# Groups of a per-element quantiser merged from the innermost outwards, over four value tiles, in a fused adapter and dense-layer kernel

## The chip, the cores and the metric

The kernel runs on one core of a Trainium2 chip. The metric is the device time of one execution in microseconds (us). TensorE is called PE (its weight loads PEld), VectorE DVE, ScalarE ACT, SyncE SP and GpSimd POOL, as in the profile.

## What is computed

The input x has 8 batches of 256 tokens with 1024 features, all in float32. Two layers follow each other:

```
# layer 0: quantise x element by element, then a mixture of 4 low-rank adapters
gi  = sum(|x| <= thresholds)             # 8 thresholds, so 0..8
idx = min(gi, 7); d = deltas[idx]; zp = zero_points[idx]
q   = (clip(round(x / d) + zp, 0, 63) - zp) * d,   but 0 where gi == 8
logits = q @ router_w.T ; gates = softmax over the best 2 of 4
x1  = x + sum over the experts of gate * (q @ A[e].T @ B[e].T) * 4
# layer 1: two dense layers, each with low-rank terms chosen per batch, one after the other
y   = x1 @ W.T + low-rank(label of the batch)
out = x1 + y @ kernel + bias + low-rank(gate of the batch) + shared low-rank
```

## The kernel before

**The products.** The two dense layers of layer 1 and the identity are multiplied with one another first: p = W.T times (kernel + shared low-rank) + identity. This takes 16 *steps* on PE (`for n in range(STEPS)`): two halves of the output columns with eight row tiles each. In the first eight steps PE has in front of the step's product a product for the per-batch low-rank part (L902, L904, the "u" product, which ACT copies out at L545). All the large products are made of three matmuls of rounded float32 parts: high by high, low by high and high by low. So every operand is split first: ACT writes the high part (for a tile of W `weight_hi`, L435), DVE subtracts to get the low part (`weight_lo`, L650, "w_lo"). Each finished step is copied from PSUM by ACT as p_hi (L533) and by DVE as p_lo (L750). Between the steps and the main part stands the product of p with the expert matrix bet (L939 to L941, 48 matmuls), which wants all p_lo parts, and bet_hi and bet_lo (L553, L763).

Then the main part: 64 more steps, numbered 16 to 79 as slots, or q = 0 to 63 in this part; eight of them for each batch b. A step of it is half of one output tile: 12 matmuls of 512 columns (L971 to L973), at its start in even steps one for the bias (L969), and in odd steps a *close* (L948, two records in the trace), in which the batch's low-rank terms (zt by tb) are added and the tile is finished. ACT then copies it out (L497) and SP stores it. In step 4 of each batch stands `z_begin` of the next one (L876, L880), and at ZEND its `z_end` (L887), whose result ACT copies to zt (L582); the close of the batch wants it.

**The quantiser.** Beside all this, ACT and DVE quantise the eight batches, one after the other, each in one piece of 128 x 2048. Per batch there are eight *groups* g, one for each threshold. ACT makes the rounded levels (`levels`, L406) and from them a clipped value (`raise_levels`, L417); DVE clips it from above and shifts it (`value`, L609), makes a mask (`mask`, L619, absx <= threshold), and merges the value into the batch's result where the mask is set (`merge`, L626). The groups go from the outermost (largest threshold) inwards, so that each overwrites the one before. At the end `finish` (L631) multiplies by absx > smallest threshold. The magnitude (L396) has one tile, absx, and waits for the `finish` of the batch before; it is made behind the raise of group 1. The tile `val` has four parts: the result of a batch is in part c % 2 (`acc`), and the values of groups 1 to 7 go round over the other two parts (`turn`). So a raise waits for the merge two groups before, and the raise of group 0 for the product of the batch two before.

PE multiplies a finished batch with the router and the adapters (`mid`, L854). DVE then ranks the logits (`order`, L691 to L700, seven small steps that each wait for the one before), ACT takes the exponential (L456), DVE makes the gates and applies them (`gate`, L707 to L713), PE turns the result round (`gated_turn`, L864), and ACT copies it to zt (`gated_out`, L462).

**The order by hand.** The engines' queues are written out in this order:

```
TAKEN = [2, 0, 2, 1, 1, 2, 1, ...]     # groups begun in each step
GROUPS[i]                              # the (batch, group) pairs of step i
DONE[c]                                # the step of batch c's last group
LAGS[c]                                # steps from DONE to mid, ranks, gate, turn, out
```

In step n DVE does first the small things (`weight_lo` for step n + 1, `p_out` of step n - 1), then GROUPS[n], then ranks and gates. In the main part ranks and gates stand ahead of the groups. ACT is one step ahead: in step n it does its small things and then levels and raises of GROUPS[n + 1].

Of the kernel before, what the change touches and what calls it, by code (L numbers as in the profile page):

```python
# [35 lines left out]
P = 128  # L36
BATCH = 8
# [26 lines left out]
def build(nc, a, out_t, itok):  # L64
# [124 lines left out]
    abs_made, levels_made, raised = sem("abs_made"), sem("levels_made"), sem("raised")  # L189
    valued, masked, merged, q_made = sem("valued"), sem("masked"), sem("merged"), sem("q_made")  # L190
    mid_made, gate_step, gap_made, exp_made = sem("mid_made"), sem("gate_step"), sem("gap_made"), sem("exp_made")
# [17 lines left out]
    AHEAD = 2  # L209
    LAGS = [(2, 3, 4, 5, 6)] * 2 + [(2, 4, 5, 6, 7)] * (BATCH - 4) + [(1, 2, 3, 4, 5)] * 2  # L210
    TAKEN = [2, 0, 2, 1, 1, 2, 1, 1, 1, 1, 1, 1, 1, 1, 1, 2, 1, 1]
    ORDER = [(c, g) for c in range(BATCH) for g in range(G)]
    SLOTS = STEPS + BATCH * KT
    LAST = STEPS + BATCH * KT - 8
    rest, room = len(ORDER) - AHEAD - sum(TAKEN), LAST + 1 - len(TAKEN)
# [5 lines left out]
    DONE = [max([-1] + [i for i in range(SLOTS) if (c, G - 1) in GROUPS[i]]) for c in range(BATCH)]  # L221
    MID, RANK, GATE, TURN, OUT = {}, {}, {}, {}, {}
    for c, d in enumerate(DONE):
        mid_at, rank_at, gate_at, turn_at, out_at = LAGS[c]
        MID[d + mid_at], RANK[d + rank_at], GATE[d + gate_at], TURN[d + turn_at] = c, c, c, c

        OUT[d + out_at if c < ZSLOTS else max(d + out_at, STEPS + (c - ZSLOTS + 1) * KT)] = c
# [32 lines left out]
    def slot(b, j):  # L260
        return STEPS + b * KT + j

    def acc(c):

        return c % 2

    def turn(c, g):

        return acc(c) if g == 0 else 2 + g % 2

# [3 lines left out]
    with nc.allow_non_contiguous_dma(reason="rows of 1 KB and small constants"), nc.Block() as block:  # L274
# [117 lines left out]
        def _(act):  # L392
            def magnitude(c):
                if c:
                    act.wait_ge(q_made, c)
                nc.scalar.activation(absx, xq[:, c % 2], ACT.Abs).then_inc(abs_made, 1)  # L396

            def levels(c, g):

                if g == 0 and c == 0:  # L400
                    act.wait_ge(x_first_in, 16)
                elif g == 0:
                    act.wait_ge(xq_in[c % 2], 16 * ((c + 1) // 2))
                if c * G + g >= 2:
                    act.wait_ge(raised, c * G + g - 1)
                nc.scalar.activation(level[:, g % 2], xq[:, c % 2], ACT.Copy, scale=inv[:, g:g + 1]).then_inc(levels_made, 1)  # L406

            def raise_levels(c, g):

                act.wait_ge(levels_made, c * G + g + 1)  # L410
                if g == 0 and c >= 2:
                    act.wait_ge(mid_made, c - 1)
                elif g >= 3:
                    act.wait_ge(merged, c * (G - 1) + g - 2)
                elif c and g:
                    act.wait_ge(merged, c * (G - 1) + 1 - g)
                nc.scalar.activation(val[:, turn(c, g)], level[:, g % 2], ACT.Relu, bias=shift[:, g:g + 1],  # L417
                                     scale=par[:, 1, g:g + 1]).then_inc(raised, 1)
# [116 lines left out]
            for n in range(STEPS):  # L535
# [39 lines left out]
            for q in range(BATCH * KT + LAG + 1):  # L575
# [17 lines left out]
                if slot(b, j) in RANK:  # L593
                    gate_exp(RANK[slot(b, j)])
                if b + 1 < BATCH and j in XAT:
# [8 lines left out]
        def _(dve):  # L604
            def value(c, g):

                dve.wait_ge(raised, c * G + g + 1)
                v = val[:, turn(c, g)]
                nc.vector.tensor_scalar(v, v, width[:, g:g + 1], unshift[:, g:g + 1], ALU.min, ALU.add).then_inc(valued, 1)  # L609

            def mask(c, g):

                if g == 1:
                    dve.wait_ge(abs_made, c + 1)
                    if c:
                        dve.wait_ge(merged, c * (G - 1))
                elif g >= 3:
                    dve.wait_ge(merged, c * (G - 1) + g - 2)
                nc.vector.tensor_scalar(inside[:, g % 2], absx, thr[:, g - 1:g], None, ALU.is_le).then_inc(masked, 1)  # L619

            def merge(c, g):
                dve.wait_ge(valued, c * G + g + 1)
                dve.wait_ge(masked, c * (G - 1) + g)
                if g >= 2:
# [60 lines left out]
            def order(c):  # L685
# [16 lines left out]
            def gate(c):  # L702

                n = c * GATE_STEPS
                mid = midbank[:, 0:TT * RT].rearrange("p (t m) -> p t m", t=TT)
                dve.wait_ge(exp_made, c + 1)
                then(nc.vector.scalar_tensor_tensor(gates, rank, TOP_K, expo, ALU.is_lt, ALU.mult), n + 8)  # L707
                then(nc.vector.reduce_sum(total, gates, AX), n + 9)
# [75 lines left out]
        def _(pe):  # L784
# [61 lines left out]
            def mid(c):  # L846

                pe.wait_ge(q_made, c + 1)
                pe.wait_ge(ra_in, 16)
# [182 lines left out]
```

## Time and profile before

| what | us |
|---|---|
| median of 3 runs | 481.31 (480.68 to 481.42) |
| the profiled execution | 477.87 |
| its span | 476.1 |
| PE busy | 461.1 |
| DVE busy | 392.2 |
| ACT busy | 358.1 |

The granted clock of PE was 1.00 of full speed throughout, so 2.4 GHz. A bracket at the end of a timeline row gives the idle time of that engine just before the instruction, and what ended it.

### The profile page before, as it was taken

Reading aid. Unit: us, or ns where it says so; the run is one execution under the profiler, and the core shown is the slowest. Engines: PE = TensorE matmul, PEld = TensorE weight load, DVE = VectorE, ACT = ScalarE, POOL = GpSimd, SP = SyncE. Lnnn points to the kernel's source line nnn. Section 1 sums busy time; section 2 is a strip of 40 time slices with the busy share of each in tenths; the row PEclk is TensorE's granted clock in tenths of the full one; section 3 lists DMA queues with packets and bytes.
Section 4 is the critical chain, followed back from the end, with each engine's and each line's share of the span. In section 5 each row is a group of like instructions: output and inputs, shape, how many; then the busy total and the mean of one; then the engine's idle time right before and its main releaser. Section 6 shows DMA issues by size and latency. Waiting matters only on the chain.

```text
span 476.1 us, 5627 instructions
## 1 busy us (share of the span) xinstructions
PE 461.1 (97%) x2182; PEld 352.9 (74%) x2182; DVE 392.2 (82%) x381; ACT 358.1 (75%) x299; POOL 5.6 (1%) x11
## 2 busy tenths in 40 slices
PE   8899989999999899999999999999999999989896
PEld 8537878888688777777777777787778768857774
DVE  1376889897999989996999799999989995999600
ACT  1499977893799986579789959968989778968002
POOL 0000010000000000000000000000000000000000
PEclk9999999999999999999999999999999999999999
DMA  8998323302143222605035106304304104101102
GB/s 270 362 361 339 75 64 136 99 12 67 43 164 124 89 45 88 200 0 156 11 134 154 56 1 187 112 1 155 144 8 149 55 1 132 56 1 44 45 0 89
DMA packets 35836, 50.35 MB, mean 106 GB/s; under 512 B 26626, under 2 KB 26882, under 8 KB 33538
## 3 DMA queue, kind: packets, MB, share of 16 engines
q1 hardware_dynamic: 34802, 42.66, 27.9%
q0 software_dynamic: 1008, 7.34, 4.1%
q8 instruction: 17, 0.28, 0.2%
q14 instruction: 9, 0.07, 0.0%
HBM read 39.51 MB, written 10.49 MB: 105 GB/s over the span
## 4 chain that ended last, share of the span: by engine, by line
PE 73%; DVE 14%; issue 4%; ACT 4%; DMA 3%; SPq 1%; DVEq 0%; ACTq 0%
PE bank L971 11%; PE bank L973 10%; PE bank L972 10%; DVE val L626 7%; PE bank L854 5%; PE bank L948 5%; PE bank L880 5%; PE bank L919 4%; PE bank L923 4%; PE bank L920 4%; PE bank L902 4%; DMA kst<-k_in 3%; PE bank L811 3%; DVE inside L619 3%; DVE val L609 2%
## 5 line engine op out<-in xcount | busy, mean ns | idle before, releaser
L417 ACT ACTIVATE val<-level,shift,small 128x2048 f32<-128x2048 int16 x64 | 133.9, 2093 | 16.2 <-DVE val L626 16.1
L626 DVE COPY_PREDICATED val<-inside,val 128x2048 f32<-128x2048 uint8 x56 | 142.8, 2550 | 0.3
L406 ACT ACTIVATE level<-xq,inv 128x2048 int16<-128x2048 f32 x64 | 127.9, 1999 | 0.8
L971 PE MATMUL bank<-p_hi,x_hi 128*128 128x512 f32 x256 | 101.8, 398 | 0.0
L973 PE MATMUL bank<-p_hi,x_lo 128*128 128x512 f32 x256 | 100.0, 391 | 0.0
L972 PE MATMUL bank<-p_lo,x_hi 128*128 128x512 f32 x256 | 99.9, 390 | 0.0
L609 DVE TENSOR_SCALAR val<-val,width,unshift 128x2048 f32<-128x2048 f32 x64 | 87.3, 1366 | 13.9 <-ACT val L417 13.5
L619 DVE TENSOR_SCALAR inside<-absx,thr 128x2048 uint8<-128x2048 f32 x56 | 72.1, 1300 | 3.9 <-ACT absx L396 3.9
L971 PEld LDWEIGHTS bank<-p_hi,x_hi 128*128 128x128 f32 x256 | 48.1, 188 | 17.0 <-issue 8.4
L973 PEld LDWEIGHTS bank<-p_hi,x_lo 128*128 128x128 f32 x256 | 48.1, 188 | 10.4
L972 PEld LDWEIGHTS bank<-p_lo,x_hi 128*128 128x128 f32 x256 | 48.1, 188 | 10.1 <-issue 0.2
L919 PE MATMUL bank<-kp_hi,w_hi 128*128 128x512 f32 x128 | 51.3, 401 | 3.1 <-DVE w_lo L650 3.1
L923 PE MATMUL bank<-kp_hi,w_lo 128*128 128x512 f32 x128 | 50.3, 393 | 0.0
L920 PE MATMUL bank<-kp_lo,w_hi 128*128 128x512 f32 x128 | 49.9, 390 | 0.0
L948 PE MATMUL bank<-tb,zt 128*128 128x512 f32 x64 | 32.6, 600 | 1.3 <-ACT zt L582 1.3
L854 PEld LDWEIGHTS bank<-ra,val 128*128 128x128 f32 x256 | 29.7, 192 | 3.9 <-DVE val L631 2.3
L854 PE MATMUL bank<-ra,val 128*128 128x68 f32 x256 | 29.6, 274 | 1.8 <-DVE val L631 1.8
L919 PEld LDWEIGHTS bank<-kp_hi,w_hi 128*128 128x128 f32 x128 | 24.1, 188 | 8.3 <-DVE w_lo L650 3.8
L902 PE MATMUL bank<-aefft,wst 128*128 128x256 f32 x128 | 29.1, 380 | 0.6 <-ACT ust L545 0.6
L880 PE MATMUL bank<-xs,ub 128*64 128x256 f32 x128 | 29.3, 382 | 0.0
L902 PEld LDWEIGHTS bank<-aefft,wst 128*128 128x128 f32 x128 | 24.1, 190 | 5.1 <-issue 1.7
L923 PEld LDWEIGHTS bank<-kp_hi,w_lo 128*128 128x128 f32 x128 | 24.0, 188 | 5.2
(91 smaller groups left out, 459.8 us busy)
## 6 DMA issues: line engine op xcount, KB each, us to landing
xs<-xt_in SPq DMA_DIRECT2D x8, 1024.0 KB, 4.9
out_t<-ost SPq DMA_DIRECT2D x16, 512.0 KB, 3.0
wst<-w_in SPq DMA_DIRECT2D x14, 512.0 KB, 3.5
xq<-xt_in POOLq DMA_DIRECT2D x7, 1024.0 KB, 6.1
la<-la_in SPq DMA_DIRECT2D x4, 512.0 KB, 5.3
lb<-lb_in SPq DMA_DIRECT2D x4, 512.0 KB, 12.7
kst<-k_in SPq DMA_DIRECT2D x4, 512.0 KB, 16.1
kst<-k_in SPq DMA_DIRECT2D x1, 2048.0 KB, 9.0
```

Source lines behind the costliest of these rows:

```text
L406: nc.scalar.activation(level[:, g % 2], xq[:, c % 2], ACT.Copy, scale=inv[:, g:g + 1]).then_inc(levels_made, 1)
L417: nc.scalar.activation(val[:, turn(c, g)], level[:, g % 2], ACT.Relu, bias=shift[:, g:g + 1], scale=par[:, 1, g:g + 1]).then_inc(raised, 1)
L609: nc.vector.tensor_scalar(v, v, width[:, g:g + 1], unshift[:, g:g + 1], ALU.min, ALU.add).then_inc(valued, 1)
L619: nc.vector.tensor_scalar(inside[:, g % 2], absx, thr[:, g - 1:g], None, ALU.is_le).then_inc(masked, 1)
L626: nc.vector.copy_predicated(val[:, acc(c)], inside[:, g % 2], val[:, turn(c, g)]).then_inc(merged, 1)
L854: last = mm(midbank[:, t * RT:(t + 1) * RT], val[:, acc(c), k, t * P:(t + 1) * P], ra[:, k], start=k == 0, stop=k == KT - 1)
L902: mm(ubank, wst[n % 2][:, o], aefft[:, o], start=o == 0, stop=False)
L919: mm(obank[n % RING], w_hi[side(n)][:, o], kp_hi[:, o], start=o == 0, stop=False)
L923: last = mm(obank[n % RING], w_lo[side(n)][:, o], kp_hi[:, o], start=False, stop=o == KT - 1)
L971: mm(o, x_hi[:, s, k, at], p_hi[:, h, k], start=False, stop=False)
L972: mm(o, x_hi[:, s, k, at], p_lo[:, h, k], start=False, stop=False)
L973: last = mm(o, x_lo[:, s, k, at], p_hi[:, h, k], start=False, stop=False)
```

## The change

**Merging.** Group g now works with threshold, delta and zero point 7 - g (`group`), so the innermost comes first. Masks are absx > threshold: each group overwrites what lies outside its own inner bound. The multiplication by absx > smallest threshold is done at once to the value of group 0 (`begin`, the same operation as `finish` was). The mask for group g + 1 is made in group g. The magnitude of batch c is made behind the raise of its group 0 and waits for the last mask of the batch before.

**Tiles.** All four parts of `val` go round. `HOMES[c]` names the part of batch c's result, and three for the other groups: three of the four, since the batch before is kept until its product. Its part is taken by group 3, whose raise waits for that product (mid_made >= c). From group 4 on a raise waits for the merge three before.

**Ranks.** The seven small steps of `order` are written so that two that don't depend on each other follow without a wait; best is taken from PSUM instead of from lg.

**Order.** TAKEN and LAST are changed; the lags stay (the exponential has one of its own, equal to that of the ranks). The groups of the steps, where they differ:

```
step          0        1    3    4        5        6
before   0.2 0.3       -   0.6  0.7      1.0 1.1  1.2
after    0.2          0.3   -   0.6 0.7  1.0      1.1 1.2
step         14       15       16
before      2.2    2.3 2.4    2.5
after        -     2.2 2.3    2.4 2.5
last group of batches 0 to 7, before: 4 11 19 30 40 51 62 72
                              after:  4 11 19 29 40 50 61 71
```

So the products of batches 3, 5, 6 and 7 come one step sooner. Batch 7's groups 1 to 7 are in steps 64, 66, 67, 68, 70, 71, 72 before, and in 64, 65, 66, 68, 69, 70, 71 after.

```diff
-    LAGS = [(2, 3, 4, 5, 6)] * 2 + [(2, 4, 5, 6, 7)] * (BATCH - 4) + [(1, 2, 3, 4, 5)] * 2
-    TAKEN = [2, 0, 2, 1, 1, 2, 1, 1, 1, 1, 1, 1, 1, 1, 1, 2, 1, 1]
+    LAGS = [(2, 3, 3, 4, 5, 6)] * 2 + [(2, 4, 4, 5, 6, 7)] * (BATCH - 4) + [(1, 2, 2, 3, 4, 5)] * 2
+    TAKEN = [1, 1, 2, 0, 2, 1, 2, 1, 1, 1, 1, 1, 1, 1, 0, 2, 2, 1]
-    LAST = STEPS + BATCH * KT - 8
+    LAST = STEPS + BATCH * KT - 9
...
+    HOMES = [[0, 1, 2, 3]]
+    for c in range(1, BATCH):
+        first, second, third, fourth = HOMES[-1]
+        HOMES.append([third, fourth, second, first])
+
     def acc(c):
-        return c % 2
+        return HOMES[c][0]
     def turn(c, g):
-        return acc(c) if g == 0 else 2 + g % 2
+        return HOMES[c][0 if g == 0 else 1 + (g - 1) % 3]
+    def group(g):
+        return slice(G - 1 - g, G - g)
...
             def magnitude(c):
                 if c:
-                    act.wait_ge(q_made, c)
+                    act.wait_ge(masked, c * (G - 1))
...
             def raise_levels(c, g):
-                if g == 0 and c >= 2:
-                    act.wait_ge(mid_made, c - 1)
-                elif g >= 3:
-                    act.wait_ge(merged, c * (G - 1) + g - 2)
-                elif c and g:
-                    act.wait_ge(merged, c * (G - 1) + 1 - g)
+                if g == 3 and c:
+                    act.wait_ge(mid_made, c)
+                elif g >= 4:
+                    act.wait_ge(merged, c * (G - 1) + g - 3)
+                elif c and g < 3:
+                    act.wait_ge(merged, c * (G - 1) + g - 2)
...
-                if c and g == 1:
+                if c and g == 0:
                     magnitude(c)
...
-                if n in RANK:
-                    gate_exp(RANK[n])
+                if n in EXP:
+                    gate_exp(EXP[n])
...
-                nc.vector.tensor_scalar(inside[:, g % 2], absx, thr[:, g - 1:g], None, ALU.is_le).then_inc(masked, 1)
+                nc.vector.tensor_scalar(inside[:, g % 2], absx, thr[:, group(g)], None, ALU.is_gt).then_inc(masked, 1)
...
-            def finish(c):
-
-                dve.wait_ge(merged, (c + 1) * (G - 1))
-                nc.vector.scalar_tensor_tensor(val[:, acc(c)], absx, thr[:, G - 1:G], val[:, acc(c)],
-                                               ALU.is_gt, ALU.mult).then_inc(q_made, 1)
+            def begin(c):
+
+                dve.wait_ge(valued, c * G + 1)
+                dve.wait_ge(abs_made, c + 1)
+                nc.vector.scalar_tensor_tensor(val[:, acc(c)], absx, thr[:, group(0)], val[:, acc(c)],
+                                               ALU.is_gt, ALU.mult).then_inc(begun, 1)
 
             def quant(c, g):
                 value(c, g)
-                if g == 1:
-                    mask(c, 1)
-                if g and g + 1 < G:
+                if g == 0:
+                    begin(c)
+                if g + 1 < G:
                     mask(c, g + 1)
                 if g:
                     merge(c, g)
-                if g + 1 == G:
-                    finish(c)
...
-                then(nc.vector.tensor_copy(lg, mid[:, :, ER:RT]), n + 1)
-                then(nc.vector.reduce_max(best, lg, AX), n + 2)
-                nc.vector.tensor_tensor(gap, lg, best.unsqueeze(2).to_broadcast([P, TT, E]), ALU.subtract).then_inc(gap_made, 1)
-                then(nc.vector.tensor_tensor(ties, other, mine, ALU.is_equal), n + 3)
-                then(nc.vector.tensor_tensor(ties, ties, before, ALU.mult), n + 4)
-                then(nc.vector.tensor_tensor(beats, other, mine, ALU.is_gt), n + 5)
-                then(nc.vector.tensor_tensor(beats, beats, ties, ALU.add), n + 6)
-                then(nc.vector.reduce_sum(rank, beats, AX), n + 7)
+                nc.vector.tensor_copy(lg, logits).then_inc(gate_step, 1)
+                nc.vector.reduce_max(best, logits, AX).then_inc(gate_step, 1)
+                dve.wait_ge(gate_step, n + 1)
+                nc.vector.tensor_tensor(ties, other, mine, ALU.is_equal).then_inc(gate_step, 1)
+                nc.vector.tensor_tensor(beats, other, mine, ALU.is_gt).then_inc(gate_step, 1)
+                dve.wait_ge(gate_step, n + 2)
+                nc.vector.tensor_tensor(gap, lg, best.unsqueeze(2).to_broadcast([P, TT, E]), ALU.subtract).then_inc(gap_made, 1)
+                dve.wait_ge(gate_step, n + 3)
+                nc.vector.tensor_tensor(ties, ties, before, ALU.mult).then_inc(gate_step, 1)
+                dve.wait_ge(gate_step, n + 5)
+                nc.vector.tensor_tensor(beats, beats, ties, ALU.add).then_inc(gate_step, 1)
+                dve.wait_ge(gate_step, n + 6)
+                nc.vector.reduce_sum(rank, beats, AX).then_inc(gate_step, 1)
...
-            value(0, 0)
-            mask(0, 1)
-            mask(0, 2)
-            value(0, 1)
-            merge(0, 1)
+            quant(0, 0)
+            quant(0, 1)
             weight_lo(1)
...
-                pe.wait_ge(q_made, c + 1)
+                pe.wait_ge(merged, (c + 1) * (G - 1))
```

## Rows read from the trace of the kernel before

**Rows 1.** The page's first part: busy time, share of the span, instructions.
```profile
PE 461.1 (97%) x2182; PEld 352.9 (74%) x2182; DVE 392.2 (82%) x381; ACT 358.1 (75%) x299; POOL 5.6 (1%) x11
```

**Rows 2.** Busy time by stretch: length, PE, PEld, DVE, ACT, POOL, clock, DMA.
```profile
232.00:268.00 36.00, 36.00 (x172) 27.21 (x171) 34.88 (x23) 33.36 (x24) 0.53 (x1) 1.00 0.30 99
```

**Rows 3.** Timeline of PE: start, length, line, operation; in brackets the idle time before.
```profile
47.48 2.83 PE L902 MATMUL bank<-aefft,wst 128*128 128x256 f32 x12 [0.57 <-ACT ust L545]
...
62.88 0.50 PE L919 MATMUL bank<-kp_hi,w_hi 128*128 128x512 f32 x1 [1.56 <-DVE w_lo L650]
...
157.37 0.50 PE L919 MATMUL bank<-kp_hi,w_hi 128*128 128x512 f32 x1 [1.58 <-DVE w_lo L650]
...
162.99 3.68 PE L854 MATMUL bank<-ra,val 128*128 128x68 f32 x32
...
178.64 0.50 PE L939 MATMUL bank<-p_hi,bet_hi 128*128 128x512 f32 x1 [0.99 <-DVE bet_lo L763]
...
189.96 0.50 PE L939 MATMUL bank<-p_hi,bet_hi 128*128 128x512 f32 x1 [0.83 <-DVE p_lo L750]
...
413.98 0.71 PE L864 MATMUL bank<-ident,mg 128*128 128x128 f32 x4 [0.19 <-DVE mg L713]
...
422.45 1.98 PE L948 MATMUL bank<-tb,zt 128*128 128x512 f32 x4 [1.26 <-ACT zt L582]
...
446.71 3.45 PE L854 MATMUL bank<-ra,val 128*128 128x68 f32 x29 [1.83 <-DVE val L631]
```

**Rows 4.** Groups of instructions: busy us, mean ns | idle before, releasers.
```profile
L626 DVE COPY_PREDICATED val<-inside,val 128x2048 f32<-128x2048 uint8 x56 | 142.8, 2550 | 0.3
L417 ACT ACTIVATE val<-level,shift,small 128x2048 f32<-128x2048 int16 x64 | 133.9, 2093 | 16.2 <-DVE val L626 16.1
...
L609 DVE TENSOR_SCALAR val<-val,width,unshift 128x2048 f32<-128x2048 f32 x64 | 87.3, 1366 | 13.9 <-ACT val L417 13.5
L619 DVE TENSOR_SCALAR inside<-absx,thr 128x2048 uint8<-128x2048 f32 x56 | 72.1, 1300 | 3.9 <-ACT absx L396 3.9
...
L631 DVE SCALAR_TENSOR_TENSOR val<-absx,thr,val 128x2048 f32<-128x2048 f32 x8 | 18.8, 2352 | 0.3
```

**Rows 5.** Timeline of DVE in the 16 steps.
```profile
47.89 1.25 DVE L650 TENSOR_TENSOR w_lo<-wst,w_hi 128x1024 fp32r<-128x1024 f32 x1
...
56.17 1.36 DVE L609 TENSOR_SCALAR val<-val,width,unshift 128x2048 f32<-128x2048 f32 x1
...
61.57 1.26 DVE L650 TENSOR_TENSOR w_lo<-wst,w_hi 128x1024 fp32r<-128x1024 f32 x1
...
156.10 1.22 DVE L650 TENSOR_TENSOR w_lo<-wst,w_hi 128x1024 fp32r<-128x1024 f32 x1
...
177.36 1.23 DVE L763 TENSOR_TENSOR bet_lo<-bet,bet_hi 128x1024 fp32r<-128x1024 f32 x1 [0.19 <-ACT bet_hi L553]
...
189.23 0.68 DVE L750 TENSOR_TENSOR p_lo<-bank,p_hi 128x512 fp32r<-128x512 f32 x1
```

**Rows 6.** Timeline of ACT in the 16 steps.
```profile
55.15 1.05 ACT L435 ACTIVATE w_hi<-wst 128x1024 fp32r<-128x1024 f32 x1
...
175.80 0.58 ACT L533 ACTIVATE p_hi<-bank 128x512 fp32r<-128x512 f32 x1
```

**Rows 7.** The chain of waits around batch 6's product: start, length, what.
```profile
394.16 0.86 PE bank L948 x2
...
401.58 3.54 PE bank L854 x32
```

**Rows 8.** Timeline of DVE in the ranks of batch 6.
```profile
405.14 0.17 DVE L691 COPY lg<-bank 128x8 f32<-128x8 f32 x1 [5.22 <-PE bank L854]
...
405.54 0.17 DVE L693 TENSOR_TENSOR gap<-lg,best 128x8 f32<-128x8 f32 x1
405.62 0.18 DVE L696 TENSOR_TENSOR ties<-lg 128x32 f32<-128x32 f32 x1
405.84 0.19 DVE L697 TENSOR_TENSOR ties<-ties,before 128x32 f32<-128x32 f32 x1
```

More of the change, by code:

```diff
@@ L189, in build @@
     abs_made, levels_made, raised = sem("abs_made"), sem("levels_made"), sem("raised")
-    valued, masked, merged, q_made = sem("valued"), sem("masked"), sem("merged"), sem("q_made")
+    valued, begun, masked, merged = sem("valued"), sem("begun"), sem("masked"), sem("merged")
     mid_made, gate_step, gap_made, exp_made = sem("mid_made"), sem("gate_step"), sem("gap_made"), sem("exp_made")
@@ L221, in build @@
     DONE = [max([-1] + [i for i in range(SLOTS) if (c, G - 1) in GROUPS[i]]) for c in range(BATCH)]
-    MID, RANK, GATE, TURN, OUT = {}, {}, {}, {}, {}
+    MID, RANK, EXP, GATE, TURN, OUT = {}, {}, {}, {}, {}, {}
     for c, d in enumerate(DONE):
-        mid_at, rank_at, gate_at, turn_at, out_at = LAGS[c]
-        MID[d + mid_at], RANK[d + rank_at], GATE[d + gate_at], TURN[d + turn_at] = c, c, c, c
+        mid_at, rank_at, exp_at, gate_at, turn_at, out_at = LAGS[c]
+        MID[d + mid_at], RANK[d + rank_at], EXP[d + exp_at], GATE[d + gate_at], TURN[d + turn_at] = c, c, c, c, c
         OUT[d + out_at if c < ZSLOTS else max(d + out_at, STEPS + (c - ZSLOTS + 1) * KT)] = c
@@ L405, in levels @@
                     act.wait_ge(raised, c * G + g - 1)
-                nc.scalar.activation(level[:, g % 2], xq[:, c % 2], ACT.Copy, scale=inv[:, g:g + 1]).then_inc(levels_made, 1)
+                nc.scalar.activation(level[:, g % 2], xq[:, c % 2], ACT.Copy, scale=inv[:, group(g)]).then_inc(levels_made, 1)
             def raise_levels(c, g):
                 act.wait_ge(levels_made, c * G + g + 1)
-                if g == 0 and c >= 2:
-                    act.wait_ge(mid_made, c - 1)
-                elif g >= 3:
+                if g == 3 and c:
[3 more added lines that the diff above has]
+                elif c and g < 3:
                     act.wait_ge(merged, c * (G - 1) + g - 2)
-                elif c and g:
-                    act.wait_ge(merged, c * (G - 1) + 1 - g)
-                nc.scalar.activation(val[:, turn(c, g)], level[:, g % 2], ACT.Relu, bias=shift[:, g:g + 1],
-                                     scale=par[:, 1, g:g + 1]).then_inc(raised, 1)
+                nc.scalar.activation(val[:, turn(c, g)], level[:, g % 2], ACT.Relu, bias=shift[:, group(g)],
+                                     scale=par[:, 1, group(g)]).then_inc(raised, 1)
             def quant(c, g):
@@ L592, in _ @@
                         quant(c, g)
-                if slot(b, j) in RANK:
-                    gate_exp(RANK[slot(b, j)])
+                if slot(b, j) in EXP:
+                    gate_exp(EXP[slot(b, j)])
                 if b + 1 < BATCH and j in XAT:
@@ L608, in value @@
                 v = val[:, turn(c, g)]
-                nc.vector.tensor_scalar(v, v, width[:, g:g + 1], unshift[:, g:g + 1], ALU.min, ALU.add).then_inc(valued, 1)
+                nc.vector.tensor_scalar(v, v, width[:, group(g)], unshift[:, group(g)], ALU.min, ALU.add).then_inc(valued, 1)
             def mask(c, g):
                 if g == 1:
-                    dve.wait_ge(abs_made, c + 1)
                     if c:
@@ L623, in merge @@
                 dve.wait_ge(masked, c * (G - 1) + g)
-                if g >= 2:
+                if g == 1:
+                    dve.wait_ge(begun, c + 1)
+                else:
                     dve.wait_ge(merged, c * (G - 1) + g - 1)
                 nc.vector.copy_predicated(val[:, acc(c)], inside[:, g % 2], val[:, turn(c, g)]).then_inc(merged, 1)
-            def finish(c):
-                dve.wait_ge(merged, (c + 1) * (G - 1))
-                nc.vector.scalar_tensor_tensor(val[:, acc(c)], absx, thr[:, G - 1:G], val[:, acc(c)],
-                                               ALU.is_gt, ALU.mult).then_inc(q_made, 1)
+            def begin(c):
[3 more added lines that the diff above has]
+                                               ALU.is_gt, ALU.mult).then_inc(begun, 1)
             def quant(c, g):
                 value(c, g)
-                if g == 1:
-                    mask(c, 1)
-                if g and g + 1 < G:
+                if g == 0:
+                    begin(c)
+                if g + 1 < G:
                     mask(c, g + 1)
@@ L690, in order @@
                 dve.wait_ge(before_in, 16)
-                then(nc.vector.tensor_copy(lg, mid[:, :, ER:RT]), n + 1)
-                then(nc.vector.reduce_max(best, lg, AX), n + 2)
-                nc.vector.tensor_tensor(gap, lg, best.unsqueeze(2).to_broadcast([P, TT, E]), ALU.subtract).then_inc(gap_made, 1)
+                logits = mid[:, :, ER:RT]
                 mine = lg.unsqueeze(3).to_broadcast([P, TT, E, E])
                 other = lg.unsqueeze(2).to_broadcast([P, TT, E, E])
-                then(nc.vector.tensor_tensor(ties, other, mine, ALU.is_equal), n + 3)
-                then(nc.vector.tensor_tensor(ties, ties, before, ALU.mult), n + 4)
-                then(nc.vector.tensor_tensor(beats, other, mine, ALU.is_gt), n + 5)
-                then(nc.vector.tensor_tensor(beats, beats, ties, ALU.add), n + 6)
-                then(nc.vector.reduce_sum(rank, beats, AX), n + 7)
+                nc.vector.tensor_copy(lg, logits).then_inc(gate_step, 1)
[11 more added lines that the diff above has]
+                nc.vector.reduce_sum(rank, beats, AX).then_inc(gate_step, 1)
             def gate(c):
@@ L706, in gate @@
                 dve.wait_ge(exp_made, c + 1)
+                dve.wait_ge(gate_step, n + 7)
                 then(nc.vector.scalar_tensor_tensor(gates, rank, TOP_K, expo, ALU.is_lt, ALU.mult), n + 8)
```

## The prediction

> **What bounds the kernel now.** I read the page's first part, then the waits of PE alone, then the timelines of PE, DVE and ACT around each of them, and last the chain of waits near the end.
>
> PE is busy for 461.1 of 476.1 us [rows 1]. In the middle it never rests: 36.00 of 36.00 us in the stretch shown [rows 2], and its clock is full. So the time is PE's own work plus the few places where it stands. The change leaves PE's work as it is; all that it can win is in those places. There are eight after the first 25 us [rows 3], and the reader should see their releasers: 0.57 for a copy of ACT, 1.56 and 1.58 for a low part of the weights (w_lo), 0.99 for bet_lo, 0.83 for p_lo, 0.19 for mg, 1.26 for zt, 1.83 for the finished batch 7 (val L631). Together 8.81. The rest of the 15.0 us without PE work lies in the first 23 us and in the last store, which the change doesn't touch.
>
> They have one cause: DVE or ACT has the quantiser's work in front of a small step that PE wants.
>
> **The change, part by part.**
>
> (1) *The work of the quantiser stays.* Per batch there are still 8 levels, 8 raises and one magnitude on ACT, and 8 values, 7 masks, 7 merges and one multiply by absx > thr on DVE. Means are in [rows 4]; the multiply (2.35 us) goes from the end of a batch (finish) to its start (begin). is_gt for is_le costs nothing: same form and tiles. Merges with dense and with sparse masks are all among the 56 of one group with mean 2550 ns, so turning the masks around costs nothing either; I bound it by the 0.15 us by which single merges differ, times the 7 of the last batch, 1 us to either side.
>
> (2) *The first wait for w_lo, 1.56.* Now step 0 has groups 0.2 and 0.3, and only then comes step 1's w_lo at 61.57 [rows 5]. PE wanted it at 62.88 less 1.56, at 61.3. After the change step 0 has 0.2 alone. DVE is free at 56.17, adds the k part (0.6), and the high part is there from 55.15 + 1.05 = 56.2 [rows 6]: w_lo is made by 58.0. Gain 1.56, with 3 us to spare. In the prelude DVE has the multiply more and one mask is moved, so w_lo of tile 1, now at 47.89 [rows 5], is begun about 1.1 later and made at 50.2 (after raise(0,1), at 44.1, come a value, a mask and a merge, 4.85, and w_lo itself, 1.25); PE wants it 3.9 after 47.48, at 51.4: 1.2 us to spare. The 0.57 stays: ACT's order there is the same.
>
> (3) *The second, 1.58.* DVE makes w_lo at 156.10, right after finish(1) [rows 5]. Finish is gone from there: 2.3 us (2.35 long, [rows 4]). All of DVE's steps before it hang on PE's and come 1.56 sooner with it, and the ranks of batch 0 save 0.4 (below). So it is made at 157.3 - 2.3 - 1.6 - 0.4 = 153.0; PE, itself 1.56 sooner, wants it at 155.8 - 1.56 = 154.2. Gain 1.58, with 1.2 to spare. What is behind: group 2.0 now has multiply and mask too, 3.5 us more ahead of the w_lo of step 14, which is made by 159.3; PE wants it only after its step 13, 5.6 (157.37 to 162.99, [rows 3]), and the product of batch 1, 3.5, so at 163.4.
>
> (4) *bet_lo, 0.99, and p_lo, 0.83.* Step 14 loses its group, so DVE has ranks, p_lo(14) and bet_lo as soon as PE's step 14 is over (163.4 + 5.6 = 169.0). bet_lo then takes 0.3 until ACT copies, 1.56 from ACT's copy at 175.80 to bet_lo at 177.36 and its own 1.23 [rows 5, 6]: 172.1, wanted at 174.6. Then two groups (4.85 each: 56.17 to 61.57 less the 0.6 of the k part) and the gate (1.0), and p_lo(15) is made at 183.4, where it now is made at 189.9 [rows 5]. PE wants it for its last three of 48 products of 0.23 us each (5.6 over the 24 of a step), so 10.2 after 174.6, at 184.8. Gain 1.82, with 1.4 to spare. ACT has to give raise(2,3) for that, which now also waits for batch 1's product (163.4): it is reached at about 166, so no wait. Up to here 4.96 us.
>
> (5) *Middle.* The products of batches 3, 5, 6 and 7 are asked one step sooner. Between the ranks of one batch and the product of the next DVE has six groups: at most 6/8 of a batch's (142.8+87.3+72.1+18.8)/8 = 40.1 [rows 4], 30.1, plus ranks and gate 2.6 and two x_lo 2.5: 35.2. PE needs 39.2 for ten steps (next point). So 4 us to spare, and no new wait; ACT's waits for merges (16.1 us, [rows 4]) get shorter with the third turning tile, but these lie beside PE's work and are worth nothing there.
>
> (6) *The end.* From the end of batch 6's product, 401.58 + 3.54 = 405.12 [rows 7], to batch 7's at 446.71 [rows 3] are 41.6 us: ten steps of PE, 38.3, and waits of 0.19, 1.26 and 1.83. DVE was ready early (5.22 idle before 405.14, [rows 8]) and then worked without a break to 446.66. After the change the stretch begins one step sooner. PE has one close more in it, 0.86 [rows 7]: 39.2. DVE has 41.5 less 2.35 (finish) less 1.20 (first mask, now in group 7.0, which fills the 5.22): 38.0. The ranks save 0.4, but with no group between them the gate waits about 0.4 for ACT's exp. So DVE is done 1.2 us before PE asks: 1.83 goes. The gate follows the ranks at once and has three steps until its turn: 0.19 goes. zt is copied in a step of ACT that now has no group ahead of it: 1.26 goes. ACT's raise(7,4) now comes after that copy, and this is the tightest point: PE's four steps with turn and z_end take 13.3, zt 0.4, a level and a raise 4.0, so 17.7 from the start of the stretch; DVE wants it after ranks and gate (2.6), three groups (14.6) and an x_lo (1.1), at 18.3. Gain 3.28.
>
> (7) *Ranks.* Two operations with a wait between start 0.22 apart (405.62 to 405.84), two without 0.08 (405.54 to 405.62) [rows 8]. Three of the seven waits lose their effect, so 0.4 us per batch.
> The Trainium skill (VectorE: DVE Perf Modes, The DRAIN you can't avoid) says that leaving semaphores out between chained VectorE operations gains nothing, and that the semaphore itself is free. By it the ranks would stay at 1.6 us and the two margins of 1.2 us would be 0.8; the sum is the same by either. The rows just named disagree with it for such small tiles.
>
> **Sum:** 1.56 + 1.58 + 0.99 + 0.83 + 0.19 + 1.26 + 1.83 = 8.24. The profiled execution took 477.87 (span 476.1); it would take 469.6. The median of the runs, 481.31, is 3.4 above it, and I take the same difference off it: 473.1.
>
> **Rivals.**
>
> *A, one of the tight places holds:* margins are 1.2 (tile 1), 1.2 (step 13), 1.4 (p_lo), 0.6 (raise(7,4)) and 1.2 (batch 7). Hand sums like these err by a microsecond or two. DVE late by 2 to 4 us in the last stretch would give back 1 to 3 us of the 8.24, w_lo late by as much again up to 1.6: 474.3 to 477.5, say 475.5. For it: five places with little room. Against: each alone would have to lose its margin first, and what it gives back is only what goes beyond it. Chance 0.27.
>
> *B, slower: the products asked too early.* Place: batches 3, 5, 6 and 7 on PE. If ACT, held at raise(c,3), which now waits for the product of the batch before, starves DVE, then this product is late, and the next raise with it. Price: a step is 3.3 us on average (two from 394.16 + 0.86 = 395.02 to 401.58, [rows 7]); four times this is 13.1, less the 8.24: 486.2. It decides from where DVE is more than 4 us later than PE's step (point 5). Against: ACT comes to raise(c,3) one to three steps after the product except in step 6, where it may wait 1 us with nothing of PE's behind. Chance 0.05.
>
> *C, nothing changes: DVE is the bound.* DVE's and ACT's busy shares are 82% and 75% [rows 1]; weight loads fill only 74% of PE's time. If PE had slack within its busy time, the fixed sum of DVE's work would set the time and reordering would bring nothing: 481.3. Against: the middle stretch, where PE takes 36.00 of 36.00 and DVE idles.
> The Trainium skill (Perfetto Trace Analysis, Identifying the Most-Contended Engine) reads PE by its weight loads, not by its matmuls' busy share. By that rule this case comes true; the trace doesn't bear it out, as PE restarts at once on each release. Chance 0.06.
>
> *D, more than the sum:* restarts after a wait cost PE some 0.1 to 0.2 us each beyond the idle time (first matmuls of 0.50 where others take 0.40), and DVE's early lead might take the 0.57 too: up to 1.5 more, 471.6. Chance 0.10.
>
> The forecast itself has 0.52.
>
> **How the numbers follow.** 473.1 is the likeliest. The range from 471.7 to 477.0 holds the forecast, D and most of A, and leaves out B, C and the end of A. About 0.2% (1 us) is what a measurement of this kernel can tell from no change. Faster by more: forecast, A, D and a little less, 0.88; within it: C, 0.06; slower: B, 0.06.
>
> **What would show it right or wrong.** PE's waits should be four: three in the first 23 us and the 0.57 at 47. No wait for w_lo at 61 and 154, none before bet_hi's products, none for zt; the product of batch 7 starts at about 435 without a wait; DVE idles less than 2 us between batch 6's product and it. PE's busy time stays within 1 us of 461. Wrong would be: a wait of PE for val L626 (A or B), for w_lo whose releaser is ACT's w_hi (A), waits of ACT for PE's product L854 ahead of L417 (B), or PE's busy time growing by what its waits lose (C).

## The result, and the profile after

The kernel after takes 468.28 us (467.90 to 468.35, 4 runs), the kernel before 481.37 in the same comparison: ratio 0.9725, interval 0.969 to 0.976, so 13.1 us less. Forecast were 473.1 and 8.2 less, with a range down to 471.7. The direction was right, the size was not, and the time lies below the range.

Page of after, parts 1 and 2 (busy time, share of the span, instructions; below, tenths of full clock in 40 slices):

```profile
span 466.1 us, 5628 instructions
...
PE 459.5 (99%) x2182; PEld 353.3 (76%) x2182; DVE 389.0 (83%) x381; ACT 356.8 (77%) x299; POOL 5.4 (1%) x11
...
PEclk9999999999999999999999999999999999999999
```

Beside [rows 1] the span is 10.0 us shorter, DVE and ACT do what they did (DVE 3 us less, most of it the ranks: with the old ones it is 391.6), and PE's busy time is 1.6 less, beyond the 1 us that the prediction allowed. These are all of PE's waits in after (engine, line, waited for: us in total, times, longest):

```profile
PE bank L802 <- DVE warm L675: 1.2, 1, 1.2
PE bank L814 <- DVE kst L667: 1.0, 1, 1.0
PE bank L915 <- ACT ust L554: 0.7, 1, 0.7
```

Of the eight waits in [rows 3] only the first is left, the 0.57, now 0.68; the prediction had a third wait in the first 23 us, of which two are left. The groups of [rows 4] in after:

```profile
L636 DVE COPY_PREDICATED val<-inside,val 128x2048 f32<-128x2048 uint8 x56 | 142.3, 2542 | 0.3
L426 ACT ACTIVATE val<-level,shift,small 128x2048 f32<-128x2048 int16 x64 | 133.9, 2091 | 2.3 <-PE bank L867 1.9
...
L618 DVE TENSOR_SCALAR val<-val,width,unshift 128x2048 f32<-128x2048 f32 x64 | 86.0, 1344 | 9.5 <-ACT val L426 9.5
```

The merge costs what it cost (2542 ns for 2550), with the masks turned round. ACT's raise waited 16.1 us for merges and now waits for one merge, 0.4; the other 1.9 is for PE's product L867 of the batch before. The last stretch, timeline of DVE and of PE in after, answers to [rows 8] and the last of [rows 3]:

```profile
395.56 0.17 DVE L703 COPY lg<-bank 128x8 f32<-128x8 f32 x1 [2.70 <-PE bank L867]
395.64 0.15 DVE L704 TENSOR_REDUCE best<-bank 128x2 f32<-128x8 f32 x1
395.76 0.19 DVE L706 TENSOR_TENSOR ties<-lg 128x32 f32<-128x32 f32 x1
...
396.50 0.18 DVE L715 TENSOR_REDUCE rank<-beats 128x8 f32<-128x32 f32 x1
...
430.59 2.48 DVE L636 COPY_PREDICATED val<-inside,val 128x2048 f32<-128x2048 uint8 x1
```
```profile
434.10 3.68 PE L867 MATMUL bank<-ra,val 128*128 128x68 f32 x32
```

DVE is done at 433.07, 37.5 after the stretch begins, and PE asks at 434.10, 38.5 after: 1.0 to spare.

The span lost 10.0 us, the waits only 8.24. Where the rest lies can be read from the starts of the same matmuls before and after. The first matmuls of steps 1 and 2, before and then after:

```profile
51.37 0.47 PE L919 MATMUL bank<-kp_hi,w_hi 128*128 128x512 f32 x1
62.88 0.50 PE L919 MATMUL bank<-kp_hi,w_hi 128*128 128x512 f32 x1 [1.56 <-DVE w_lo L650]
```
```profile
51.17 0.48 PE L932 MATMUL bank<-kp_hi,w_hi 128*128 128x512 f32 x1
60.90 0.48 PE L932 MATMUL bank<-kp_hi,w_hi 128*128 128x512 f32 x1
```

The same work takes 11.51 us before and 9.73 after, so the wait shown as 1.56 was worth 1.78. The whole span, cut at such starts:

| stretch | before, us | after, us | less by | waits in it before |
|---|---|---|---|---|
| up to step 1 | 51.37 | 51.17 | 0.20 | (0.57, stays) |
| step 1 to step 2 | 11.51 | 9.73 | 1.78 | 1.56 |
| to step 13 | 94.49 | 92.74 | 1.75 | 1.58 |
| to the product with bet | 21.27 | 19.94 | 1.33 | 0.99 |
| to the main part | 17.48 | 16.58 | 0.90 | 0.83 |
| to the end | 279.97 | 275.96 | 4.01 | 0.19, 1.26, 1.83 |

From step 1 on that is 9.8 us for waits of 8.24: 1.5 more over seven places, some 0.2 for each stop. Stretches without a wait are as long as before (steps 2 to 8: 64.16 and 64.15). PE's ends are modelled, so how much of it counts as busy is open; the starts aren't.

### The profile page after: what moved, and what is told of

The parts are those of the page before. It is cut to its first block, busy times and chain, and to the rows that moved or that the text cites. A ratio compares the mean times of both kernels' runs of the same rounds, so it can differ in the third digit from the quotient of the medians.

```text
span 466.1 us, 5628 instructions
## 1 busy us (share of the span) xinstructions
PE 459.5 (99%) x2182; PEld 353.3 (76%) x2182; DVE 389.0 (83%) x381; ACT 356.8 (77%) x299; POOL 5.4 (1%) x11
## 4 chain that ended last, share of the span: by engine, by line
PE 87%; ACT 4%; DMA 3%; DVE 2%; issue 2%; SPq 1%; ACTq 0%
PE bank L984 13%; PE bank L986 13%; PE bank L985 13%; PE bank L961 6%; PE bank L893 6%; PE bank L867 5%; PE bank L915 5%; PE bank L936 5%; PE bank L932 5%; PE bank L933 5%; DMA kst<-k_in 3%; PE bank L824 3%; PE bank L889 2%; PE bank L982 2%; ACT level L415 1%
## 5 line engine op out<-in xcount | busy, mean ns | idle before, releaser
L636 DVE COPY_PREDICATED val<-inside,val 128x2048 f32<-128x2048 uint8 x56 | 142.3, 2542 | 0.3
L618 DVE TENSOR_SCALAR val<-val,width,unshift 128x2048 f32<-128x2048 f32 x64 | 86.0, 1344 | 9.5 <-ACT val L426 9.5
L867 PEld LDWEIGHTS bank<-ra,val 128*128 128x128 f32 x256 | 29.7, 192 | 1.4 <-issue 1.0
L867 PE MATMUL bank<-ra,val 128*128 128x68 f32 x256 | 29.5, 273 | 0.0
L933 PEld LDWEIGHTS bank<-kp_lo,w_hi 128*128 128x128 f32 x128 | 24.1, 188 | 5.0 <-issue 0.2
```

The source lines that it names most:

```text
L618: nc.vector.tensor_scalar(v, v, width[:, group(g)], unshift[:, group(g)], ALU.min, ALU.add).then_inc(valued, 1)
L867: last = mm(midbank[:, t * RT:(t + 1) * RT], val[:, acc(c), k, t * P:(t + 1) * P], ra[:, k], start=k == 0, stop=k == KT - 1)
L933: mm(obank[n % RING], w_hi[side(n)][:, o], kp_lo[:, o], start=False, stop=False)
```

## Where the other 5 us came from: the kernel before, profiled again

The sum of the prediction was made against one profiled execution of 477.87 us. The first question was what its distance to the median is.

> The kernel before, unchanged, profiled again. Its profiled execution on record took 477.9 us, its other executions 480.7 to 482.9. Theory 1 (the ordinary execution of before has more or longer waits of PE than the one profiled): a second profile has a span of about 479.5 and PE waits for DVE and ACT that add up to some 3 us more than the 8.8 after the first 25 us, PE busy still 461. Theory 2 (the difference is PE's own pace, the transfers or the chip): the same eight waits with the same lengths, and the time lies in PE's busy time, in the first 25 us or in the clock. Theory 3: the span is 476 again and the difference lies outside the span.

Measured: span 480.7, mean clock 0.989. PE's waits are the same eight, with the same lengths within 0.12 us. PE's busy time is 466.1 instead of 461.1, and the place is one. Timeline of PE, then busy time by stretch (length, PE, PEld, DVE, ACT, POOL, granted clock, DMA):

```profile
446.47 6.35 PE L854 MATMUL bank<-ra,val 128*128 128x68 f32 x32 [1.76 <-DVE val L631]
```
```profile
440.00:446.40 6.40, 4.72 (x21) 3.57 (x19) 6.33 (x4) 0.00 (x0) 0.00 (x0) 1.00 0.20 82
446.40:457.00 10.60, 10.53 (x43) 9.56 (x44) 2.33 (x14) 0.21 (x1) 0.00 (x0) 0.54 0.01 2
457.00:470.00 13.00, 13.00 (x58) 10.20 (x57) 0.00 (x0) 0.76 (x2) 0.00 (x0) 0.98 0.00 1
```

After PE has waited for the finished batch 7, the clock falls from 2.4 to 1.2 GHz. The product of 32 short matmuls takes 6.35 us. The clock is back after 10.2 us; half of these are lost. In the execution on record the same wait of 1.83 was followed by full clock, and the product took 3.79 (the row in [rows 3] shows only 29 of its 32 matmuls).

Each execution's record has its mean clock, and the comparisons of this and the later runs have 51 executions of the kernel before. One, at 0.982 and 486.25 us, stands apart from the other 50. By clock: 8 at 1.00, median 478.1 us; 3 at 0.996, 479.9; 26 at 0.992 or 0.993, median about 481.3; 13 at 0.989, median 482.9. The 0.989 is the case profiled here, 10.2 us at half clock; a mean of 0.993 over 480 us is worth 0.007 x 480 / 0.5 = 6.7 us of it, and 0.996 half as much. The profile on record was of the rare kind, at full clock. Theory 2 holds: not more waits, but the clock. Between executions at full clock, 478.1 and 468.3, the change is worth 9.8 us; the other 3.3 are what the median of before has on top. Where the clock fell in the executions at 0.992 and 0.993 no profile shows; that it is the same place follows only from the next two runs.

The Trainium skill (TensorE: Matmul & The Clock Gate, Part 1) describes these two levels and a monitor of activity that sets them. The levels agree with the profile: 0.50 and 1.00 of full speed.

## Is it that one wait? Taken away from before, put into after

```diff
-    LAGS = [(2, 3, 4, 5, 6)] * 2 + [(2, 4, 5, 6, 7)] * (BATCH - 4) + [(1, 2, 3, 4, 5)] * 2
+    LAGS = [(2, 3, 4, 5, 6)] * 2 + [(2, 4, 5, 6, 7)] * (BATCH - 4) + [(1, 2, 3, 4, 5), (2, 3, 4, 5, 6)]
```

> The kernel before with batch 7's product and all that hangs on it one step later, nothing else. Theory (the clock): PE's wait of 1.8 us ahead of that product is what lets the granted clock fall to half for 6.8 or 10.2 us in 19 of 23 executions so far, at a cost of 3.4 or 5.1 us on top. Without the wait the clock stays at 1.00 in every execution and the median falls from 481 to 474.5 to 475, 6 us for a wait of 1.8. Rival: the clock falls for the sum of PE's pauses, or whatever it does there: it still falls in most executions, and the median is 1.8 less, about 479.

Measured: 475.72 us (475.23 to 477.56, 6 runs), ratio 0.989 (0.985 to 0.993), clock 1.00 in five and 0.996 in one. In that one, which was profiled, the 3.4 us at half clock lie between 25 and 30 us of the span, among the start's products, not at the end. The wait before batch 7's product is gone and the other seven stand. A wait of 1.8 us was worth 5.7 in the median: 2.4 between executions at full clock (478.1 and 475.7), the rest lost clock. The theory holds. (The expectation counts 19 of 23 executions with a fall; the record has 18.)

The reverse: after, with DVE work ahead of batch 7's last merge (masks that nobody reads).

```diff
             def quant(c, g):
...
+                if (c, g) == (7, G - 1):
+                    dve.wait_ge(merged, c * (G - 1) + g - 1)
+                    dve.wait_ge(valued, c * G + g + 1)
+                    for i, n in enumerate([KT] * 2 + [2]):
+                        nc.vector.tensor_scalar(inside[:, 0, 0:n], val[:, turn(c, g), 0:n], 0.0, None, ALU.is_gt).then_inc(spent, 1)
+                        dve.wait_ge(spent, i + 1)
                 if g:
                     merge(c, g)
```

> The kernel after with 2.8 us of DVE work added ahead of the last merge of batch 7 (masks of a value that nobody reads). DVE had 1.0 us to spare there, so PE waits about 1.8 us for the product. Theory (the clock): it falls to half there in most executions, median 468.3 + 1.8 + 3.4 = 473.5 or more, single ones at 470.1 with clock 1.00. Rival (the fall needs the other waits of before too): all executions at 470.1.

Measured: 474.52 us (473.52 to 475.37, 6 runs), clock 0.989 or 0.993 in all six. PE's timeline, and the stretch behind the wait:

```profile
436.32 6.66 PE L874 MATMUL bank<-ra,val 128*128 128x68 f32 x32 [1.85 <-DVE val L637]
```
```profile
436.80:447.10 10.30, 10.30 (x40) 9.38 (x40) 2.00 (x13) 0.69 (x2) 0.00 (x0) 0.50 0.13 52
```

So the added DVE work (2.95 us in the trace) cost 6.2, of which 1.85 is the wait. With less work (`[KT] + [2]`):

> As the kernel with a wait of 1.85 us ahead of batch 7's product, but with 1.6 us of added DVE work instead of 2.8: a wait of about 0.6 us. Theory (length of the pause matters): the clock stays at 1.00 in most executions, median 468.9. Rival (any pause just ahead of the short matmuls does it): clock 0.989 to 0.993, median 472 or more.

Measured: 469.61 us (468.63 to 472.22, 6 runs), wait 0.61, clock 0.998 or more in four, 0.996 and 0.993 in the others. The profiled one is that at 0.996, and its fall lies before 30 us again (23.3 to 26.7). So the pause's length matters at this place: a third of it mostly kept the clock. The same work ahead of the last merge of batch 1 (`[KT] * 2 + [6]`) makes PE wait at a place where full matmuls follow:

> The kernel after with 3.4 us of the same DVE work ahead of the last merge of batch 1, so that w_lo of step 13 comes late: PE waits about 2 us ahead of a step of full matmuls. In before no execution seen lost its clock after such a wait (1.56 and 1.58). Theory (it matters what follows: after the wait for batch 7 come 32 short matmuls of 68 columns, here 24 of 512): clock 1.00, median 468.3 + 2.0 = 470.3. Rival (any pause of 1.8 us or more does it): clock below 1, median 473.5. If the p_lo or bet_lo waits come back by less than 1 us, that is the margin of the prediction's point 4 used up.

Measured: 472.99 us (470.70 to 474.02, 6 runs). The wait is 2.49, longer than meant (w_lo comes 3.5 us later, and in after it had only 0.8 to spare), and the clock was 1.00 in two executions, 0.996 in three, 0.993 in one. The profiled one is at 1.00 and has full clock right behind the wait:

```profile
156.38 0.50 PE L939 MATMUL bank<-kp_hi,w_hi 128*128 128x512 f32 x1 [2.49 <-DVE w_lo L666]
```

Neither theory holds as stated. A longer pause than batch 7's cost less clock here. Where the clock fell in the other four executions isn't shown, as only one is profiled. It need not be behind this wait: kernels without any such wait also have executions at 0.996 or 0.993 (two of four with the old ranks, below).

All the profiles together say more than this run alone. Eleven pauses of 1.5 to 2.7 us stand ahead of products of 512 columns (w_lo and bet_lo, in seven profiles), and no fall of the clock begins behind any of them. Of the four pauses of 1.76 to 2.41 ahead of batch 7's product three were followed by one. So was each of two pauses for p_lo, of 1.85 and 1.79 in two kernels of the next section; behind these stand three matmuls of 512 columns and then 32 of 64 and 256. The place matters, then, and it isn't what PE did just before: ahead of step 13 and ahead of batch 7's product alike it had been at 512 columns. What it is in the short matmuls (their columns, or their weight loads) was not separated. It isn't the pauses of before at 414 and 422 [rows 3] either: the kernel with the 1.85 has none of them.

## The parts of the change by themselves

**The order alone** (TAKEN and LAST of after; merging, tiles and ranks of before):

```diff
-    TAKEN = [2, 0, 2, 1, 1, 2, 1, 1, 1, 1, 1, 1, 1, 1, 1, 2, 1, 1]
+    TAKEN = [1, 1, 2, 0, 2, 1, 2, 1, 1, 1, 1, 1, 1, 1, 0, 2, 2, 1]
-    LAST = STEPS + BATCH * KT - 8
+    LAST = STEPS + BATCH * KT - 9
```

> The kernel before with TAKEN and LAST of after, merging, tiles and ranks as before. If the parts add up as in the prediction's steps: the first w_lo wait (1.56), bet_lo and p_lo (1.82) and zt and mg (1.45) go; the second w_lo wait stays at about 1.5, since finish(1) is still ahead of it; the wait for batch 7's product stays and is 2 to 2.5 us, since DVE has 41.5 us of work there against 39.2 of PE. Profiled span about 471 to 472, ratio to before about 0.990. Rival (handing out the groups does all of it): as after, ratio 0.973. Rival (order is worth nothing without the new merging): 1.00.

Measured: 490.36 us (488.80 to 490.90, 4 runs), ratio 1.020 (1.013 to 1.026): slower than before by 9. Two waits came where they were expected, 2.27 for w_lo of step 13 (about 1.5 expected) and 2.41 for batch 7. The 1.85 for p_lo was expected to be gone. A fourth was in no sum. Timelines of ACT and PE:

```profile
190.60 1.99 ACT L406 ACTIVATE level<-xq,inv 128x2048 int16<-128x2048 f32 x1
198.40 2.09 ACT L417 ACTIVATE val<-level,shift,small 128x2048 f32<-128x2048 int16 x1 [5.81 <-DVE val L626]
200.52 1.08 ACT L486 ACTIVATE tb<-bank 64x512 f32<-64x512 f32 x2
201.50 0.21 ACT L478 ACTIVATE bu<-bank 64x64 f32<-64x64 f32 x1
```
```profile
201.76 1.11 PE L887 MATMUL bank<-zt,bu 64*64 64x256 f32 x2 [5.21 <-ACT bu L478]
```

ACT is at raise(2,6), the raise of batch 2's group 6, which wants the merge two groups before, and DVE, with groups 2.2 and 2.3 later than before, hasn't come to it. Behind the raise stands the copy of bu, which z_end multiplies, and PE waits 5.21 for it. The p_lo is late in the same way: ACT's p_hi of step 15 stands behind raise(2,5), at 186.23 to 188.33. Around the wait for bu the clock falls too:

```profile
196.00:202.00 6.00, 0.79 (x4) 0.34 (x3) 6.00 (x4) 3.29 (x4) 0.00 (x0) 0.94 0.90 298
202.00:210.00 8.00, 8.00 (x25) 5.83 (x25) 5.86 (x4) 2.46 (x5) 0.00 (x0) 0.62 0.04 7
```

It is at half for 6.8 us there, from 201.3, just before PE starts again; for 3.4 us from 191.0, behind the wait for p_lo; and for 6.8 us from 453.9, behind that for batch 7. Half of that, some 8 us, is lost. Against before's profiled execution at full clock the span is 12.0 longer, so most of it is clock.

**The new order without the third turning tile** (the tile stays, the raises wait as if there were two):

```diff
                 elif g >= 4:
-                    act.wait_ge(merged, c * (G - 1) + g - 3)
+                    act.wait_ge(merged, c * (G - 1) + g - 2)
```

> The kernel after with the raises of groups 4 to 7 waiting for the merge two before, as with two turning tiles, all else as after. The prediction said that the third turning tile is worth nothing on PE. But the new order with the old tiles had ACT stand 5.8 us at raise(2,6) for merge(2,4), behind it bu, and PE waited 5.2 for bu. Theory (the tile carries the new order): this wait comes back here, PE waits some 3 to 5 us ahead of z_end(0), and the clock may fall after it; ratio 0.985 to 1.00. Rival (the tile is worth nothing, what hurt there was finish): as after, ratio 0.973.

Measured: 479.90 us (478.34 to 481.93, 10 runs), ratio 0.997 (0.994 to 1.000); waits of 5.24 for bu and 1.79 for p_lo, no other after 50 us, clock 0.985 to 0.993. In the profiled one it is at half for 3.4 us behind the wait for p_lo and for 6.8 us around that for bu. So one part of `val` carries 11.6 us of after's time, 7 of them waits and most of the rest clock. Under the old order of groups it is another matter. First the new merging and all tiles with the old order:

> The kernel after with TAKEN and LAST of before: new merging, four tiles and new ranks alone. By the prediction's steps: the first w_lo wait (1.56) and most of bet_lo and p_lo (1.8) stay, the second w_lo wait, zt and the wait for batch 7's product go (1.58, 1.26, 1.83). Profiled span about 471, ratio about 0.990. If instead the product of batch 7 is still waited for, the DVE sum of the last stretch (38 us) is wrong. Rival (merging alone does all): ratio 0.973.

Measured: 473.16 us (472.62 to 473.68, 4 runs), ratio 0.985 (0.978 to 0.991), clock 0.999 or more in all. Span 470.8 as expected; these waits are left after 50 us and the ones for the second w_lo and for batch 7 are gone:

```profile
PE bank L932 <- DVE w_lo L659: 1.5, 1, 1.5
...
PE bank L952 <- DVE bet_lo L776: 1.2, 1, 1.2
PE bank L952 <- DVE p_lo L763: 0.9, 1, 0.9
...
PE bank L961 <- ACT zt L591: 0.2, 1, 0.2
```

And the same with the line above at g - 2:

> New merging with the old order of groups, raises of groups 4 to 7 waiting for the merge two before. With the third turning tile this order had a span of 470.8. Theory (the tile carries the new order only; under the old one it saves ACT waits that PE never sees): span within 0.5 of 470.8, no wait for bu, ratio 0.984. Rival (the tile is worth as much here as under the new order): PE waits for bu, ratio near 1.00.

Measured: 474.38 us (473.91 to 475.16, 4 runs), span 472.8. No wait for bu. But 2.0 in the span where I expected under 0.5: the wait for bet_lo is 2.73 instead of 1.18, as ACT's bet_hi stands behind such a raise as well (it waits 2.36 at 174 us), and 0.5 more lies in the first 37 us, which the tile doesn't touch. So the tile is worth 1.2 (medians) to 1.4 us under the old order and 11.6 under the new.

**The small parts.** After with LAST of before:

> The kernel after with LAST of before (groups of batch 7 over one step more, its product a step later). By the prediction's sums DVE and PE are level in the last stretch either way. The old-order run had only a wait of 0.2 for zt there, so: span 466.3, median as after within 0.3. Rival: the earlier product is what keeps the clock up or hides zt, and this is 1 us or more slower.

Measured: 468.63 us (468.29 to 470.68, 4 runs), span 466.5, a wait of 0.24 for zt: level with after. After with the old ranks:

> The kernel after with the ranks' seven steps each waiting for the one before, as in before. My account: 0.4 us of DVE per batch, hidden everywhere, since the last stretch has some 1 us to spare: the same as after, ratio 0.973, no new wait. Rival (the margin is used up): a wait for batch 7's product of up to 0.5 us, ratio 0.974. Either way DVE's ranks take 1.58 us from first start to last start plus 0.2, against some 1.2 in after.

Measured: 468.76 us (467.95 to 471.62, 4 runs), span 466.2. No wait after 50 us. The two executions at clock 0.999 and 1.00 took 467.95 and 467.99; the others had 0.996 and 0.993, for which nothing in the one profile gives a cause. Level with after.

**One wait more.** After with the levels of (0, 2) behind the first copy of ust:

```diff
             weight_hi(1)
-            levels(0, 2)
...
                     nc.scalar.activation(ust[:, n % 2], ubank, ACT.Copy).then_inc(u_made, 1)
+                    if n == 0:
+                        levels(0, 2)
```

> The kernel after with the levels of group (0, 2) behind the copy of the first u product instead of ahead of it. PE's last wait after the first 25 us (0.68 for ust at 47) goes, the levels come 0.3 us later, and value(0,2) had to wait for ACT anyway, so DVE shifts by about 0.3 with margins of more than 1 us. Profiled span 465.4, median 467.6 against 468.3. Rival: the raise of (0, 2) late by 0.4 us moves w_lo of step 2 or the zt copies and it is level with after.

Measured: 467.46 us (467.25 to 468.61, 6 runs), ratio to before 0.973 (0.970 to 0.976); span 465.7, and PE's only waits are those of 1.20 and 1.35 in the first 23 us. It is the lowest median here, 0.8 under after's, about the size of the wait taken away (0.68); the two were not run in one comparison.

## Why the prediction was right, and where it failed

**The step that failed is the transfer from the profile to the median**: "The median of the runs, 481.31, is 3.4 above it, and I take the same difference off it". That difference was no property of the measurement. It was the lost clock behind the 1.83 us wait, and it went with the wait. After's four executions (467.90 to 468.35) all have a clock of 0.999 or 1.00, and the profiled one is among them. The place in the sum is the term of 1.83 for batch 7, which measured 5.7 in the median when it alone was taken away. This step is about 3.1 of the 4.8 us between the forecast of 473.1 and 468.3.

**A second term was put at nothing: what a stop costs PE beyond its idle time.** It makes up most of the rest, 10.0 us of span against 8.24. By the starts of the same matmuls the seven places gave back 1.5 us more than their waits, some 0.2 each; 0.2 more lies before step 1. Rival D had this cost, "some 0.1 to 0.2 us each", at a chance of 0.10, and about that is what the places gave. Its time of 471.6 was just outside the stated range and, with the same 3.4 taken off, still too long.

The rest of the mechanism was right and not luck: the seven waits that were to go went, at the times forecast.

Point by point:
- (1) Merges of turned masks cost the same: 2542 for 2550 ns.
- (2) w_lo of step 2: forecast 58.0, made at 57.8. w_lo of tile 1: 50.2, made at 50.0. The 0.57 stayed.
- (3) w_lo of step 13: forecast 153.0, made at 152.8; 0.8 to spare instead of 1.2, since PE came 0.6 sooner than forecast. The cause was right: the order alone, with finish still there, left this wait, at 2.27.
- (4) bet_lo 172.1, made at 172.5; p_lo(15) 183.4, made at 183.9. Of the 1.4 to spare for p_lo nothing was left: PE's matmuls before it start 0.23 apart, up to 183.55, and the next one at 184.00, so PE stood about 0.2 there, too little for the list of waits.
- (5) "worth nothing there" about the third turning tile was wrong as a statement on the change. It holds for the middle steps: with the raises waiting as for two tiles PE has no wait after 198 us either. But points 3, 4 and 6 were summed with it in place, in the new order, and without it ACT blocks at raise(2,6) for 5.8 us. I priced the tile where the old trace showed ACT's waits instead of asking what the new order would do without it.
- (6) DVE 38.0, measured 37.5; PE 39.2, measured 38.5; 1.2 to spare, measured 1.0. All three waits went. "The earlier product" itself (LAST) did nothing.
- (7) Ranks: now 0.94 from first to last start (395.56 to 396.50), before 1.58. That is 0.6 saved instead of 0.4, and worth nothing in time, as said. Two without a wait start 0.08 to 0.12 apart.

Rival A didn't come, but p_lo had nothing left. Rival C is refuted: DVE's work is the same and the time isn't. Rival B's mechanism, ACT held at a raise and PE waiting for what stands behind, is real (its chance is 0.05 in one sentence of the prediction and 0.06 in another). It waits for a merge, not for the product of the batch before, and it appears as soon as the third tile is taken away: 479.9, and 490.4 with finish there too.

## What to carry to other kernels

Where the median differs from the profiled execution, look at the clock of every execution before carrying the difference over. A pause of TensorE of under 2 us may cost three times its length, so its price is not its own length. And an order of work and the buffers that it needs are one change: here the order alone lost 9 us, the buffers and merging alone won 8, and together they won 13. The 9 and the 13 both hold some us of clock: a wait that an order makes or takes away brings its clock with it.

## What the runs showed of the hardware that I had not expected

- The clock fell to 1.2 GHz behind a pause of 1.8 us, for 10.2 us where it was profiled, in most executions but not in all of the same program (42 of 50 of before had a mean below 1.00). Behind a pause of 0.61 at the same place it mostly stayed, and behind none of eleven profiled pauses of 1.5 to 2.7 ahead of 512-column matmuls did it fall. PE's busy time grows by it (461.1 to 466.1) without any new wait, so a list of waits doesn't show it; the clock of the stretch does.
- It can also fall for 3.4 us among the start's products, at 23 to 28 us, in single executions: two profiles of this study have it.
- A stop of PE costs some 0.2 us beyond the idle time that the profile shows (9.8 us for seven waits of 8.24).
- Of two small VectorE operations the second starts 0.08 to 0.12 us after the first where it doesn't wait, and 0.19 to 0.23 where it does.
